# A graph transformer block over 32 groups of graphs: attention probabilities normalised in place on VectorE instead of a turned table of row sums, and the output projection from high and low parts

## The reference, cut to what matters

```python
nx = _ln(x, ln1_g, ln1_b)
q = (nx @ wq + bq).reshape(b, s, H, HD).transpose(0, 2, 1, 3)
k = (nx @ wk + bk).reshape(b, s, H, HD).transpose(0, 2, 1, 3)
v = (nx @ wv + bv).reshape(b, s, H, HD).transpose(0, 2, 1, 3)
adjf = adj_matrix.astype(jnp.float32)
bias = jnp.where(adj_matrix > 0, 0.1 * edge_attr_matrix * adjf, -jnp.inf)[:, None]
scores = jnp.einsum('bhqd,bhkd->bhqk', q, k) / np.sqrt(HD) + bias
attn = jax.nn.softmax(scores, axis=-1)
out = jnp.einsum('bhqk,bhkd->bhqd', attn, v)
out = out.transpose(0, 2, 1, 3).reshape(b, s, d)
x1 = residual + (out @ wo + bo)
n2 = _ln(x1, ln2_g, ln2_b)
mlp = jax.nn.gelu(n2 @ w1 + b1, approximate=False) @ w2 + b2
return x1 + mlp
```

## Time and profile before

| | |
|---|---|
| Median of three runs | 1585.09 us |
| The profiled execution: its own time | 1585.44 us |
| Its span | 1583.6 us |
| Granted TensorE clock, mean over the span | 0.995 |
| TensorE (PE) busy | 96%, 12604 matmul instructions |
| ScalarE (ACT) busy | 73%, 3335 |
| VectorE (DVE) busy | 64%, 2129 |
| GpSimd (POOL) busy | 31%, 392 |
| DMA | 29 GB/s over the span |

### The profile page before, as it was taken

The page is one execution under the profiler, slowest core; times in us unless marked ns, Lnnn a source line. Parts: engine busy times, 40 slices in busy tenths (PEclk is TensorE's granted clock), DMA queues, the critical chain, the costliest instruction groups (busy, mean ns, idle before and its releaser), DMA issues.

```text
span 1583.6 us, 36063 instructions
## 1 busy us (share of the span) xinstructions
PE 1526.3 (96%) x12604; PEld 1297.7 (82%) x12604; DVE 1011.0 (64%) x2129; ACT 1149.1 (73%) x3335; POOL 486.9 (31%) x392
## 2 busy tenths in 40 slices
PE   6799999999999999999999999999999999999988
PEld 5578888888888888888888888888888888888777
DVE  4666666766666756666656666666666666666553
ACT  3777777777777777777777678777778777778772
POOL 3332333312333213333213333213333223333100
PEclk9999999999999999999999999999999999999999
DMA  3101110001111011110001111011100011100000
GB/s 127 41 2 34 35 33 30 9 28 34 35 34 32 7 31 33 33 33 30 8 31 34 36 32 33 5 34 33 33 30 22 16 34 34 33 30 14 5 15 27
DMA packets 55142, 46.69 MB, mean 29 GB/s; under 512 B 3344, under 2 KB 54800, under 8 KB 55056
## 3 DMA queue, kind: packets, MB, share of 16 engines
q1 hardware_dynamic: 55056, 45.38, 9.1%
HBM read 28.58 MB, written 16.78 MB: 29 GB/s over the span
## 4 chain that ended last, share of the span: by engine, by line
PE 74%; ACT 10%; DVE 10%; issue 6%; DVEq 0%; DMA 0%; POOL 0%; ACTq 0%; SPq 0%; POOLq 0%
PE work L330 17%; PE work L332 16%; PE work L331 15%; PE area L450 8%; PE turned L408 6%; ACT soft L626 5%; PE area L437 5%; DVE soft L788 4%; PE area L390 3%; DVE nmax L792 2%; PE turned L468 2%; DVE xt_lo L886 2%; ACT probt L617 2%; PE area L421 2%; ACT hid L680 1%
## 5 line engine op out<-in xcount | busy, mean ns | idle before, releaser
L626 ACT ACTIVATE soft<-soft,nmax 128x128 f32<-128x128 f32 x1024 | 396.2, 392 | 83.8 <-DVE nmax L792 83.7
L894 DVE TENSOR_TENSOR hid_parts<-hid,hid_parts 128x512 fp32r<-128x512 f32 x256 | 215.0, 851 | 142.5 <-ACT hid_parts L687 142.5
L330 PE MATMUL work<-w_hi,hid_parts 128*128 128x256 f32 x1024 | 294.9, 288 | 1.4 <-DVE res L905 1.0
L977 POOL TENSOR_TENSOR ve<-mv,eps 128x4 f32<-128x4 f32 x64 | 12.9, 202 | 904.7 <-DVE mv L852 473.7
L332 PE MATMUL work<-w_hi,hid_parts 128*128 128x256 f32 x1024 | 285.6, 279 | 0.0
L331 PE MATMUL work<-w_lo,hid_parts 128*128 128x256 f32 x1024 | 285.3, 279 | 0.0
L680 ACT ACTIVATE hid<-work,b_col 128x512 f32<-128x512 f32 x256 | 178.0, 695 | 73.1 <-PE work L332 69.7
L330 PE MATMUL work<-nt_hi,w_hi 128*128 128x512 f32 x512 | 224.2, 438 | 1.9 <-DVE nt_lo L886 1.7
L788 DVE TENSOR_TENSOR soft<-area,ebias 128x1024 f32<-128x1024 f32 x128 | 155.7, 1216 | 96.9 <-PE area L390 96.8
L332 PE MATMUL work<-nt_hi,w_lo 128*128 128x512 f32 x512 | 201.7, 394 | 0.0
L330 PEld LDWEIGHTS work<-w_hi,hid_parts 128*128 128x128 f32 x1024 | 191.9, 187 | 11.7 <-issue 5.9
(11 more groups left out here) (87 smaller groups left out, 3000.1 us busy)
## 6 DMA issues: line engine op xcount, KB each, us to landing
xin<-in_x SPq DMA_DIRECT2D x32, 512.0 KB, 4.0
out<-res SPq DMA_DIRECT2D x128, 128.0 KB, 1.7
adj_in<-in_adj SPq DMA_DIRECT2D x32, 256.0 KB, 4.1
w_raw<-in_L_gnn_w SPq DMA_DIRECT2D x1, 1024.0 KB, 8.1
soft<-in_L_gnn_w SPq DMA_DIRECT2D x1, 1024.0 KB, 10.4
wa_raw<-in_L_gnn_wq SPq DMA_DIRECT2D x1, 256.0 KB, 3.9
wa_raw<-in_L_gnn_wk SPq DMA_DIRECT2D x1, 256.0 KB, 4.3
wa_raw<-in_L_gnn_wv SPq DMA_DIRECT2D x1, 256.0 KB, 5.4
```

The source lines that it names most:

```text
L330: pe.matmul(o, lhs_hi, rhs_hi, start=first, stop=False)
L626: a = act.activation(soft[:, b % 2, h, :], soft[:, b % 2, h, :], ACT.Exp, bias=nmax[:, b % 2, h:h + 1], accum_out=rsum[:, b % 2, h:h + 1])
L894: dve.tensor_tensor(hid_lo[:, m, :], hid[:, m % 3, :], hid_hi[:, m, :].bitcast(F32), ALU.subtract).then_inc(hid_lo_ready, 1)
```

## The change

`invert` becomes `normalise`: after the eight exponentials VectorE takes the reciprocals of the 8 row sums and multiplies all 8 x 128 probabilities of a row by them, in place in `soft`. `turn` then waits for that (`normed`) instead of for the exponentials. `spread`, `shares_copy`, `share` and their tiles are gone. The mixed values, already normalised, are split into two parts: `attn_hi` (ScalarE) copies `mixed` to the float32r tile `at_hi`, `attn_lo` (VectorE) takes the difference, `at_lo`. `project_out` is now made of the three float32r products of `three`, and for that the output weights are split too, once, in step -1. The calls in the three `body` functions are placed anew: `mix(0)` ahead of `turn(1)`, the `nt` flips ahead of both `values`, `turn(2)` behind them, `mix(2)` behind `up(0)`, `turn(3)` behind `up(1)`; on ScalarE and VectorE the copies follow.

The diff, without the declarations, the step -1 splits and the shifted counts:

```diff
--- before.py
+++ after.py
...
@@ -398,38 +395,25 @@
 
                 if b == 0 and step.has(1):
                     pe.wait_ge(taken["xt"], step.count(1, DC, DC - 1))
-                if b == 3 and step.has(-1):
+                if b == 2 and step.has(-1):
                     pe.wait_ge(taken["nt"], step.count(-1, DC, DC - 1))
                 if step.steady or step.n > 0 or b > 0:
                     pe.wait_ge(turned_taken, step.upto(0, b - 1, 2))
+                pe.wait_ge(normed, step.upto(0, b))
                 for half in range(2):
-                    pe.wait_ge(prob_ready, step.upto(0, b, 2) - (1 - half))
                     for j in range(4):
                         mm = pe.transpose(turned[:, half, j * P:(j + 1) * P],
                                           soft[:, b % 2, half * 4 + j, :], ident[:, :])
                     mm.then_inc(turned_full, 1)
...
-            def spread(step, b):
-                if not step.has(0):
-                    return
-
-                pe.wait_ge(sum_spread, step.upto(0, b))
+            def mix(step, b):
+                if not step.has(0):
...
+
                 pe.wait_ge(scores_taken, step.upto(0, min(b + 1, GB - 1)))
                 if step.steady or step.n > 0 or b > 0:
-                    pe.wait_ge(shares_taken, step.upto(0, b - 1))
-                for c in range(DC):
-                    mm = pe.transpose(shares[:, c * P:(c + 1) * P], rwide[:, b % 2, c, :, :].rearrange(
-                        "p g d -> p (g d)"), ident[:, :])
-                mm.then_inc(shares_full, 1)
-
-            def mix(step, b):
-                if not step.has(0):
-                    return
-                par = step.parity_of(0)
-
-                pe.wait_ge(scores_taken, step.upto(0, min(b + 1, GB - 1)))
-                if step.steady or step.n > 0 or b > 0:
-                    pe.wait_ge(at_ready, step.upto(0, b - 1))
+                    pe.wait_ge(at_taken, step.upto(0, b - 1))
...
@@ -445,10 +429,12 @@
 
                 if step.steady or step.n > 0 or b > 0:
                     pe.wait_ge(x1_summed, step.upto(0, b - 1))
-                pe.wait_ge(at_ready, step.upto(0, b))
+                if not step.steady and step.n == 0 and b == 0:
+                    pe.wait_ge(lo_made, 4)
+                pe.wait_ge(at_taken, step.upto(0, b))
                 for c in range(DC):
-                    mm = pe.matmul(wout, at[:, b % 2, c, :], wa_raw[:, 3, c, :], start=(c == 0),
-                                   stop=(c == DC - 1))
+                    mm = three(wout, at_hi[:, b % 2, c, :], at_lo[:, b % 2, c, :], wa_hi[:, 3, c, :],
+                               wa_lo[:, 3, c, :], c == 0, c == DC - 1)
...
@@ -542,33 +528,29 @@
                 down(step, 2)
                 turn(step, 0)
                 query_key(step, 0)
-                spread(step, 0)
+                mix(step, 0)
                 turn(step, 1)
-                mix(step, 0)
                 down(step, 3)
 
                 score(step, 2)
                 query_key(step, 1)
                 mix(step, 1)
-                spread(step, 1)
                 project_out(step, 0)
                 query_key(step, 2)
                 score(step, 3)
                 query_key(step, 3)
-                turn(step, 2)
-                values(step, 0)
                 flip(step, "nt", 0)
                 flip(step, "nt", 1)
-                spread(step, 2)
+                values(step, 0)
                 values(step, 1)
+                turn(step, 2)
+                project_out(step, 1)
+
+                up(step, 0)
                 mix(step, 2)
-                project_out(step, 1)
-
-                up(step, 0)
+                up(step, 1)
                 turn(step, 3)
-                up(step, 1)
                 up(step, 2)
-                spread(step, 3)
                 up(step, 3)
                 mix(step, 3)
...
@@ -625,15 +610,17 @@
                 for h in range(H):
                     a = act.activation(soft[:, b % 2, h, :], soft[:, b % 2, h, :], ACT.Exp,
                                        bias=nmax[:, b % 2, h:h + 1], accum_out=rsum[:, b % 2, h:h + 1])
-                    if h % 4 == 3:
-                        a.then_inc(prob_ready, 1)
-
-            def shares_copy(step, b):
-                if not step.has(0):
-                    return
-
-                act.wait_ge(shares_full, step.upto(0, b))
-                act.activation(share_rows[:, b % 2, :], shares, ACT.Copy).then_inc(shares_taken, 1)
+                a.then_inc(prob_ready, 1)
+
+            def attn_hi(step, b):
+                if not step.has(0):
+                    return
+
+                if step.steady or step.n > 0 or b > 1:
+                    act.wait_ge(wout_full, step.upto(0, b - 2))
+                act.wait_ge(mixed_full, step.upto(0, b))
+                act.activation(at_hi[:, b % 2, :, :], mixed.rearrange("p (c q) -> p c q", c=DC),
+                               ACT.Copy).then_inc(at_hi_taken, 1)
...
                 query_key_copy(step, 2)
                 query_key_copy(step, 3)
-                turned_copy(step, 2)
-                values_copy(step, 0)
                 flip_hi(step, "nt")
                 exponential(step, 3)
+                values_copy(step, 0)
                 values_copy(step, 1)
-                shares_copy(step, 2)
+                turned_copy(step, 2)
 
                 gelu(step, 0)
+                hidden_hi(step, 0)
+                attn_hi(step, 2)
...
-            def invert(step, b):
-                if not step.has(0):
-                    return
-
-                dve.wait_ge(prob_ready, step.upto(0, b, 2))
+            def normalise(step, b):
+                if not step.has(0):
+                    return
+
+                dve.wait_ge(prob_ready, step.upto(0, b))
                 dve.reciprocal(rinv[:, b % 2, :], rsum[:, b % 2, :]).then_inc(sum_inverted, 1)
                 dve.wait_ge(sum_inverted, step.upto(0, b))
-                dve.tensor_copy(rwide[:, b % 2, :, :, :], rinv[:, b % 2, :].rearrange(
-                    "p (g c a) -> p c g a", c=DC, a=1).to_broadcast([P, DC, RPB, HD])).then_inc(sum_spread, 1)
-
-            def share(step, b):
-                if not step.has(0):
-                    return
-
-                dve.wait_ge(mixed_full, step.upto(0, b))
-                dve.wait_ge(shares_taken, step.upto(0, b))
-                if step.steady or step.n > 0 or b > 1:
-                    dve.wait_ge(wout_full, step.upto(0, b - 2))
-                dve.tensor_tensor(at[:, b % 2, :, :], mixed.rearrange("p (c q) -> p c q", c=DC),
-                                  share_rows[:, b % 2, :].rearrange("p (c q) -> p c q", c=DC), ALU.mult).then_inc(at_ready, 1)
+                dve.tensor_tensor(soft[:, b % 2, :, :], soft[:, b % 2, :, :],
+                                  rinv[:, b % 2, :].rearrange("p (h a) -> p h a", a=1).to_broadcast([P, H, P]),
+                                  ALU.mult).then_inc(normed, 1)
+
+            def attn_lo(step, b):
+                if not step.has(0):
+                    return
+
+                dve.wait_ge(at_hi_taken, step.upto(0, b))
+                dve.tensor_tensor(at_lo[:, b % 2, :, :], mixed.rearrange("p (c q) -> p c q", c=DC),
+                                  at_hi[:, b % 2, :, :].bitcast(F32), ALU.subtract).then_inc(at_taken, 1)
...
+                attn_lo(step, 1)
                 residual(step, 0)
-                invert(step, 2)
                 softmax(step, 3)
+                normalise(step, 2)
                 flip_lo(step, "nt")
                 stats1(step)
-                invert(step, 3)
-                share(step, 2)
+                normalise(step, 3)
```

78 lines of the change are left out of this document (41 added, 37 removed).

## The result

The changed kernel takes 1562.11 us (median of four runs, 1560.28 to 1563.58), the kernel before 1584.3 beside it (four runs); the ratio is 0.986 (95% interval 0.9848 to 0.9872). It is faster by 22 us; the forecast was 1546.5 us, 38.6 less than before.

The account below looks back on a forecast made before the run. TensorE's own work was taken as the bound (busy 1526.3 of 1583.6 us). Saving 1.33 us in each of 29 steps, 38.6 in all, gave a span of 1545.0 and a median of 1546.5; range 1540 to 1553, 8-in-10 range 1539 to 1561.

Parts of the forecast that it names:

- Whatever is taken off it counts in full, 32 times over, unless a wait takes its place: TensorE's own work sets the time, so work removed there counts fully in all 32 steps unless waits replace it.
- So per step 1.48 - 0.10 - 0.05 = 1.33 us less: Per step: 1.48 us of TensorE work saved, less 0.10 for `mix(0)` and 0.05 for handovers of `up(0)` and `mix(2)`.
- The room that "just fits": TensorE's margins against other engines: `turn(0)` and `up(0)` just fit, with 0.05 us at `up(0)`; `turn(2)` has 0.13.
- the list of new waits: TensorE's waits in step order, `turn(0)` to `project_out(3)`; 0.20 charged every second step at `mix(0)`, 0.05 for `up(0)` and `mix(2)`.
- Removed: 3 x 0.22 + 0.37 = 1.03 us per step: TensorE's `spread` transposes: 0.22 us each pair, 0.37 right behind a `mix`; removing them saves 1.03 us per step.
- Removed: 2 x 0.86 + 2 x 1.06 = 3.84: Float32 `project_out` on TensorE: 0.86 us, or 1.06 right behind a `mix`, two of each; removal saves 3.84 per step.
- Added: 4 x 0.71 + 2 x 0.20 = 3.24: Split projection on TensorE: six matmuls take 0.71 us, plus 0.20 behind a `mix`; adds 3.24 per step.
- Steps 0, 1 and 31 ... at nothing together, between 3 us more and 4 us less: Steps lacking `up` or `query_key` to hide VectorE's longer road: counted as nothing, from 3 us more to 4 less.
- The only idle time with some size is 1.5 to 1.7 us in every second step: TensorE in the kernel before: sizeable idle time only at the loop's edge, 1.5 to 1.7 us, with no engine waited for.
- GpSimd wins the port: At `turn(0)`, the product starts late behind GpSimd; 0.84 us stays in 14 inner steps, 12 us, giving 1558; chance 0.13.
- ScalarE's middle is late: At `up(0)`, delayed exponentials of graph 3 count in full; at 0.5 us, 14.5 us in all, giving 1561; chance 0.15.
- The weight loads show: In `project_out`, weight loads set the matmul distance; 0.33 us per step slower than before, 9.6 us, giving 1595; chance 0.05.

Follow-up runs that it names:

- e10: The changed kernel with GpSimd's long addition made to wait for VectorE's last low part, `hidden_lo(7)`, of the group two back: 1538.45 us, ratio 0.9733.
- e9: The kernel before with GpSimd's long addition made to wait for VectorE's last low part, `hidden_lo(7)`, of the group two back: 1552.53 us, ratio 0.9795.
- e13: e9 without the eight `spread` transposes per step; the table is copied untransposed, so mixed values are scaled wrongly: 1540.15 us, ratio 0.9726.
- e14: e10 with the output projection back in plain float32: 1543.68 us, ratio 0.9743.
- e15: e10 with `result(3)` between the bias add and the maxima of graph 2 on VectorE: 1526.67 us, ratio 0.9643.
- e1: The changed kernel with the projection back to two float32 matmuls per graph and VectorE's low part gone: 1567.86 us, ratio 0.9908.
- e2: The changed kernel's arithmetic in the order of calls of the kernel before, on all engines: 1638.27 us, ratio 1.0334.
- e3: The changed kernel with the product written to an unread tile and transposes waiting for four exponentials at a time: 1560.66 us, ratio 0.9861.
- e7: The changed kernel with reciprocals and product made in two halves of four heads, each with its own wait: 1565.35 us, ratio 0.9877.
- e12: e2 with the product written to an unread tile and transposes waiting for four exponentials at a time: 1567.12 us, ratio 0.9893.
- e16: e10 with `turn(2)`, its copy and product back ahead of the `nt` flips in step 31 alone: 1532.3 us.
- e5: The changed kernel with `down(3)` ahead of `mix(0)` and `turn(1)`, and `result(3)` ahead of `attn_lo(0)` on VectorE: 1547.84 us, ratio 0.9782.
- e6: e5 with `project_out(1)` also moved ahead of `turn(2)`: 1548.68 us, ratio 0.977.
- e4: The changed kernel with `result(3)` between the bias add and the maxima of graph 2 on VectorE: 1556.96 us, ratio 0.9849.
- e11: e5 with GpSimd's long addition made to wait for `hidden_lo(7)` of the group two back: 1544.11 us, ratio 0.9739.
- e8: The kernel before with the split projection alone, keeping the table of row sums and its transposes: 1574.77 us, ratio 0.9926.

## Why the prediction was wrong

The direction was right, and so were several mechanisms: TensorE's own work is most of the time, the product takes 1.22 us and wins the port, the moves cover it, the split projection starts every 0.12 us. The size was off by 16 us. The step that failed is the one from work to time: *"Whatever is taken off it counts in full, 32 times over, unless a wait takes its place"*, with *"So per step 1.48 - 0.10 - 0.05 = 1.33 us less"* as all that waits were to cost. Of the 1.48, 0.50 did not come, not 0.15: the greater part went into waits of TensorE that the sum had as room or did not have at all.

The starts of the units show it. All kernels of this table have the added wait, so that the two waits at the step's start are out of it; it holds for the steps without the collision of e10, and its numbers repeat from step to step within 0.04 us. The forecast is the prediction's sum before its charges for waits, divided by place (in order: -0.22 - 0.20 + 0.15; -0.37 - 0.86 + 0.91; -0.44 - 1.06 + 0.71 + 0.20; -1.92 + 1.62). The stretches left out differ by 0.02 at most. *e10 - e9* is the whole change, *e13 - e9* the table's transposes alone, *e10 - e14* the split projection alone.

| Stretch of a step | forecast | e10 - e9 | e13 - e9 | e10 - e14 |
|---|---|---|---|---|
| `turn(0)` to `score(2)` | -0.27 | -0.16 | -0.12 | 0.00 |
| `score(2)` to `score(3)` | -0.32 | -0.10 | -0.19 | -0.03 |
| end of `query_key(3)` to `mix(3)` | -0.59 | -0.36 | -0.07 | -0.04 |
| `mix(3)` to the end of the step | -0.30 | -0.37 | 0.00 | -0.37 |
| the step | -1.48 | -0.98 | -0.37 | -0.45 |

1. *The room that "just fits"*. In the last stretch no unit starts right behind another engine in this way, and the forecast held, with 0.07 to spare. In the third, 0.23 are missing. The prediction had 0.13 us of room at `turn(2)` and 0.05 at `up(0)`, and charged 0.05 for the latter and `mix(2)`. In e10 and in the changed kernel alike, in all of the steps 3 to 28, `turn(2)` starts 0.05 us behind VectorE's last low part and `up(0)` 0.05 us behind ScalarE's first copy of values: both are waits, too short to leave TensorE idle in its rows. In the second, 0.22 are missing. `query_key(2)` waits in the same way for `result(3)`, and the list of new waits did not have it; e15 gives 0.14 of it back. From e10:

```profile
823.51 0.41 DVE L895 TENSOR_TENSOR res<-work,res 128x256 f32<-128x256 f32 x1
823.98 0.50 PE L328 MATMUL work<-xt_hi,wa_hi 128*128 128x512 f32 x1
830.21 1.28 DVE L876 TENSOR_TENSOR nt_lo<-turned,nt_hi 128x512 fp32r<-128x512 f32 x2
831.55 0.33 PE L405 MATMUL turned<-ident,soft 128*128 128x128 f32 x1
```

In the first stretch 0.11 are missing: in these steps the matmuls of `down(3)` start 0.118 apart where e9 has 0.113; e13 shows the same. No wait is named, and the cause is open. Together 0.50, of which 0.15 were charged: 0.35 per step, 10 us.

2. *"Removed: 3 x 0.22 + 0.37 = 1.03 us per step"*, for `spread`. Alone and in the old order it measured 0.37. The sum itself took 0.20 back under "Added", for the projection that now stands right behind a `mix`, so 0.83 is what to compare. Of the 0.46 that are missing, 0.37 are the two waits for `gelu` above. In the new order, with `mix(2)` between `up(0)` and `up(1)`, these waits do not occur, so this loss is the old order's and not the changed kernel's.
3. *"Removed: 2 x 0.86 + 2 x 1.06 = 3.84"* and *"Added: 4 x 0.71 + 2 x 0.20 = 3.24"*, for the projection: 0.60 forecast, 0.45 measured with the added wait, 0.42 without it (e1). Behind `mix(3)` two projections gave 0.37 where 0.30 were forecast. The other two gave 0.07: the units behind them, `query_key(2)` and `up(0)`, are those that wait.
4. *"Steps 0, 1 and 31 ... at nothing together, between 3 us more and 4 us less"*: measured +2.67, -0.22 and +2.90, with 0.38 ahead of them. In step 0 the first product is waited for in full. TensorE's waits there, of the changed kernel:

```profile
45.75 1.94 PE L405 MATMUL turned<-ident,soft 128*128 128x128 f32 x8 [4.62 <-DVE soft L794]
```

In the kernel before two waits of 1.41 and 0.81 stand there. The granted clock of the stretch is lower too, 0.73 instead of 0.89: TensorE is granted 1.2 GHz instead of 2.4 for about 20 us of it, where it was 7.5. Stretches of step 0, of the kernel before and after (length, busy times, clock, DMA share, GB/s):

```profile
36.45:70.64 34.19, 28.04 (x241) 21.40 (x241) 20.40 (x43) 22.48 (x84) 11.23 (x9) 0.89 0.07 24
```
```profile
36.83:73.69 36.86, 28.28 (x240) 22.77 (x241) 24.29 (x43) 23.08 (x84) 11.92 (x9) 0.73 0.07 22
```

I had named the reason ("no `up` or no `query_key` to hide the longer road") and then let the bounds lie on both sides of zero. The reason had only one sign.

5. *"The only idle time with some size is 1.5 to 1.7 us in every second step"*: misread from three starts. Of 15 loop edges six have such a stall in that profile, and ordinary steps, which are the many, had two waits of 0.28 and 0.36 that three rows did not show. This did not change the sum, since the waits cost 1.0 us in both kernels: the kernels without the added wait differ by 1.01 per step, those with it by 0.98. But it hid the largest gain to be had.

The rivals: *GpSimd wins the port* did not occur in the changed kernel, where all but a few of the 128 products take 1.22 us: the margin of 0.13 us held. With the wait added, the edge rows come later and the products do collide. In every second step both first products are long, which costs 0.22 per such step and not the 0.84 of the rival; in the others only the second is, at no cost to the step:

```profile
765.44 1.65 DVE L794 TENSOR_TENSOR soft<-soft,rinv 128x1024 f32<-128x1024 f32 x1
768.79 1.92 DVE L794 TENSOR_TENSOR soft<-soft,rinv 128x1024 f32<-128x1024 f32 x1
```

*ScalarE's middle is late* came true in small: `up(0)` starts on ScalarE's heels in every step, which costs about 0.1 us and not the 0.5 of the rival. *The weight loads show* did not: the projection behind a `mix`, in the changed kernel with the wait, starts every 0.12 us after the first:

```profile
777.50 0.39 PE L328 MATMUL area<-wa_hi,at_hi 128*128 128x256 f32 x1
777.72 0.28 PE L329 MATMUL area<-wa_lo,at_hi 128*128 128x256 f32 x1
777.84 0.28 PE L330 MATMUL area<-wa_hi,at_lo 128*128 128x256 f32 x1
777.96 0.28 PE L328 MATMUL area<-wa_hi,at_hi 128*128 128x256 f32 x1
```

The first distance is 0.22: at this place the projection behind narrow matmuls pays 0.10 of the 0.20 that the sum had for it.

## What to carry to other kernels

Work taken off a dense engine was priced well where no other engine was near, and came back in part where one was: of 1.48 us per step, 0.50 did not count, although in most of these steps TensorE's own rows named no wait. So a margin of 0.05 to 0.13 us is a wait to be charged, not room, once 0.3 us are taken off ahead of it. Such waits have no row of their own on TensorE. They show as a unit that starts the same 0.05 us behind the end of the instruction that releases it, step after step, or as idle time of the weight loads.

To price a part, take it out alone and compare the starts of the units stretch by stretch: the total of e13 (0.37) says little about `spread`, since two new waits hide in it. List the waits of a whole ordinary step on the engine that bounds, not only the large ones: here two waits of 0.3 us per step, set by a port collision on another engine that cost it 1.4 us, were worth more than the change when they were removed. Where a change lengthens a road and the pipeline's first and last steps have nothing to lay beside it, charge them the full length with one sign.

## What was not expected of the hardware

- *Stalls at the loop's edge go with instruction packets.* The nine profiles without such stalls (e1, e2, e3, e7, e10, e12 to e15) have 19 or 20 packets in the row `q8 instruction`; the others 28 (e16, one stall), 37 (e5, two), 47 (e9, three), 55 (after and e6, four), 56 (e4, four), 73 and 74 (e11 and before, six) and 137 (e8, 13): about nine for each. In the changed kernel's trace the nine begin 4.7 to 6.4 us ahead of each stalled `score(0)` (the first at 300.8 for the one at 305.5) and spread over the turn of the loop behind it. Which is cause and which is effect, and what decides how many there are, is open. In the kernel before, one costs 49.49 + 46.67 - 2 x 47.65 = 0.86 us, since it covers the wait behind it. Without that wait it costs more: in e11 47.68 + 47.42 - 2 x 45.8 = 3.5 at most, and its loop takes 15 us more than e10's at the same ordinary step.
- *Which of the two comes first, by 0.07 us, decides who pays.* In e10 GpSimd has a one-input instruction beside the first product of a step in the loop. In every second step it starts 0.05 us ahead of the product:

```profile
765.39 1.50 POOL L1031 TENSOR_SCALAR adj_in<-adj_in 128x512 f32<-128x512 int32 x1
```

It takes its usual 1.50, and the product of 765.44 ends at 767.09, 0.43 late; blocked to GpSimd's end it would have ended at 768.11. In the other steps the product comes 0.02 ahead, at 811.23, takes 1.22, and GpSimd's instruction takes 1.06 more:

```profile
811.25 2.56 POOL L1031 TENSOR_SCALAR adj_in<-adj_in 128x512 f32<-128x512 int32 x1
```

In e9 the table's copy took 0.71 instead of 0.29 and ended 0.74 ahead of the one-input GpSimd instruction that had started 0.05 before it. Where both had two inputs, one waited for the other's end to 0.2 us (2.08 us above). The rule of the Trainium skill, page "SBUF — State Buffer", section "SBUF: two separate sides", fits that case and the one in which VectorE is first; a one-input GpSimd instruction that is first holds VectorE up for less than its own length. Why is not shown, and the times of GpSimd's instructions are the roughest of the profile.
